# Copying the maxima into the score banks for two key tiles at a time

## What is computed

```python
q = jnp.einsum('bnd,hde->bhne', query, Wq) * scale
k = jnp.einsum('bmd,hde->bhme', query, Wk)
v = jnp.einsum('bmd,hde->bhme', query, Wv)
logits = jnp.einsum('bhne,bhme->bhnm', q, k)
attn = jax.nn.softmax(logits, axis=-1)
out = jnp.einsum('bhnm,bhme->bnhe', attn, v)
```

## Time and profile before

| what | us |
|---|---|
| two timed runs | 1841.31 and 1842.32, median 1841.82 |
| the profiled execution, device time | 1841.39 |
| its span, first to last instruction | 1839.7 |
| PE busy | 1743.4 (95% of the span) |
| POOL busy | 1338.3 (73%) |
| ACT busy | 1318.1 (72%) |
| DVE busy | 1207.4 (66%) |
| granted TensorE clock, mean | 0.994 of full speed |

### The profile page before, as it was taken

One profiled execution on the slowest core, in us unless ns is written; L12 is line 12 of the kernel. 1 busy time (PEld: TensorE's weight loads), 2 busy tenths in 40 slices (PEclk: granted clock), 3 DMA queues, 4 the chain that ended last, 5 costly groups with the idle time before them and its releaser, 6 DMA issues.

```text
span 1839.7 us, 29397 instructions
## 1 busy us (share of the span) xinstructions
PE 1743.4 (95%) x10380; PEld 1074.3 (58%) x10380; DVE 1207.4 (66%) x2155; ACT 1318.1 (72%) x1608; POOL 1338.3 (73%) x711
## 2 busy tenths in 40 slices
PE   7999999999999999999999999999999998999998
PEld 4555555555665555556655555556655454598887
DVE  5666666666676657766665667767666668665565
ACT  3787777776668777776667877776677867665775
POOL 2798888887766867798668778897668787642664
PEclk9999999999999999999999999999999999999999
DMA  4411111113322111133222111132221111543441
GB/s 132 152 47 41 47 41 47 44 57 97 115 78 64 33 41 47 46 105 125 67 67 66 41 44 44 54 106 61 70 69 50 39 58 58 178 121 115 156 138 35
DMA packets 142932, 137.72 MB, mean 75 GB/s; under 512 B 60740, under 2 KB 121284, under 8 KB 141764
## 3 DMA queue, kind: packets, MB, share of 16 engines
q1 hardware_dynamic: 139716, 127.38, 22.9%
q0 software_dynamic: 3072, 8.46, 1.3%
HBM read 102.70 MB, written 29.69 MB: 72 GB/s over the span
## 4 chain that ended last, share of the span: by engine, by line
PE 57%; ACT 12%; POOL 11%; issue 9%; DVE 8%; DMA 2%; SPq 1%; POOLq 0%; ACTq 0%; DVEq 0%
PE av_ps L1200 13%; PE score_ps L1184 11%; POOL prob_sum L1058 9%; PE spare_ps L1160 6%; PE spare_ps L1144 5%; ACT score_ps L1303 4%; PE y_ps L1782 4%; PE spare_ps L441 4%; ACT probs L1295 4%; PE h_ps L1753 4%; PE spare_ps L1137 4%; PE spare_ps L1211 3%; DVE max_of L1361 2%; DVE o_lo L513 2%; DMA x<-x 1%
## 5 line engine op out<-in xcount | busy, mean ns | idle before, releaser
L1058 POOL TENSOR_TENSOR prob_sum<-prob_sum,probs 128x1024 f32<-128x1024 f32 (+1 forms) x384 | 905.4, 2358 | 189.6 <-ACT probs L1295 154.2
L1361 DVE TENSOR_REDUCE max_of<-spare_ps 128x1 f32<-128x512 f32 x1024 | 655.8, 681 | 254.3 <-PE spare_ps L1160 244.7
L1295 ACT ACTIVATE probs<-score_ps 128x1024 f32<-128x1024 f32 x512 | 498.3, 1023 | 326.5 <-PE score_ps L1184 318.7
L1303 ACT ACTIVATE score_ps<-shift_all 128x1024 f32<-128x1024 f32 x510 | 503.7, 1031 | 0.0
L1200 PE MATMUL av_ps<-probs,v 128*64 128x512 f32 x2048 | 488.2, 602 | 0.7 <-DVE sums L1404 0.7
L1160 PE MATMUL spare_ps<-k_hi,q_hi 64*128 64x512 f32 x1024 | 238.4, 456 | 51.2 <-DVE max_of L1361 34.0
L1200 PEld LDWEIGHTS av_ps<-probs,v 128*64 128x64 f32 x2048 | 129.8, 136 | 239.8 <-issue 198.5
L1160 PEld LDWEIGHTS spare_ps<-k_hi,q_hi 64*128 64x128 f32 x1024 | 101.1, 183 | 271.3 <-issue 207.5
L1054 POOL TENSOR_TENSOR prob_sum<-probs 128x1024 f32<-128x1024 f32 (+1 forms) x64 | 150.4, 2350 | 112.1 <-ACT probs L1295 111.9
L1184 PE MATMUL score_ps<-q_hi,k_hi 64*128 64x512 f32 x1024 | 212.0, 406 | 5.9 <-ACT score_ps L1303 5.9
L1184 PE MATMUL score_ps<-q_hi,k_lo 64*128 64x512 f32 x1024 | 204.4, 390 | 0.0
(11 more groups left out here) (279 smaller groups left out, 2298.1 us busy)
## 6 DMA issues: line engine op xcount, KB each, us to landing
shift_all<-shifts SPq DMA_DIRECT2D x64, 512.0 KB, 3.7
o_transposed<-sums SPq DMA_DIRECT2D x64, 256.0 KB, 2.5
v<-in_L_ffn_W_dram SPq DMA_DIRECT2D x16, 1024.0 KB, 5.7
o_in<-o_transposed SPq DMA_DIRECT2D x28, 512.0 KB, 4.1
w_raw<-in_L_attn_Wq_dram SPq DMA_DIRECT2D x64, 64.0 KB, 2.3
w_raw<-in_L_attn_Wk_dram SPq DMA_DIRECT2D x64, 64.0 KB, 2.2
wv_raw<-in_L_attn_Wv_dram SPq DMA_DIRECT2D x32, 128.0 KB, 2.9
shifts<-neg_rows SPq DMA_DIRECT2D x256, 1.0 KB
```

The costliest lines, as they stand in the source:

```text
L1058: pool.tensor_tensor(out, out, probs[:, n % RING, heads], ALU.add).then_inc(prob_added, 1)
L1295: act.activation(probs[:, n % RING], score_ps[n % 2][:, :, :], ACT.Exp).then_inc(probs_ready, 1)
L1303: act.activation(score_ps[n % 2][:, :, :], shift_all[:, u % 2], ACT.Copy).then_inc(seeded, 1)
L1361: dve.tensor_reduce(max_of[:, u % 2, kh, j, hd:hd + 1], bank[:, :], AX.X, ALU.max).then_inc(pass_read, 1)
```

## The change

The table loses one "seed" of two in each place, so that one remains after each pair of exponentials. The two score buffers become halves of one PSUM tensor of four banks. `seed(n)`, called for even n, waits for `probs_ready` n (was n - 1), which is the end of `exp(n - 1)`, the instruction just ahead of it on ACT; it copies the same 1024 maxima twice, 2048 columns in one instruction, into all four banks, and then adds 2 to `seeded`. What `score(n)` waits for is unchanged in the code (`seeded` n - 1). There are 255 such copies in place of 510.

```diff
-    "early av av av pass score score seed seed pass sum av recip pass score score seed seed pass late bite bite",
+    "early av av av pass score score seed pass sum av recip pass score score seed pass late bite bite",
...
-            if name == "seed" and h < HALVES and KT * u + kt + 2 < KT * UNITS:
-                yield "seed", KT * u + kt + 2
+            if name == "seed" and h < HALVES and KT * u + KH * second + 2 * i + 2 < KT * UNITS:
+                yield "seed", KT * u + KH * second + 2 * i + 2
...
-        score_ps = [ctx.enter_context(nc.psum_tensor(f"score_ps{i}", [P, 2, BANK], F32)) for i in range(2)]
+        score_banks = ctx.enter_context(nc.psum_tensor("score_ps", [P, 2, 2, BANK], F32))
+        score_ps = [score_banks[:, i] for i in range(2)]
...
-                act.wait_ge(probs_ready, n - 1)
-                act.activation(score_ps[n % 2][:, :, :], shift_all[:, u % 2], ACT.Copy).then_inc(seeded, 1)
+                act.wait_ge(probs_ready, n)
+                both = shift_all[:, u % 2]
+                act.activation(score_banks[:, :, :, :], bass.AP(both.tensor, both.offset, [both.ap[0], (0, 2), (1, 2 * BANK)]),
+                               ACT.Copy).then_inc(seeded, 2)
```

More of the change, by code:

```diff
@@ L658 @@
 STEPS = tuple(tuple(line.split()) for line in (
-    "early av av av pass score score seed seed pass sum av recip pass score score seed seed pass late bite bite",
-    "bite norm pass score score seed seed pass early av av pass score score seed seed pass late av av",
-    "av pass score score seed seed pass early av sum pass score score seed seed pass bite late av recip av",
-    "pass norm score score seed seed pass early bite bite av pass score score seed seed pass late av av av"))
+    "early av av av pass score score seed pass sum av recip pass score score seed pass late bite bite",
+    "bite norm pass score score seed pass early av av pass score score seed pass late av av",
+    "av pass score score seed pass early av sum pass score score seed pass bite late av recip av",
+    "pass norm score score seed pass early bite bite av pass score score seed pass late av av av"))
 def bites_of(g, quarter, pairs):
```

## The result

| | before | after |
|---|---|---|
| timed runs, median | 1841.82 us | 1916.59 us (1916.56 and 1916.61) |
| ratio | | 1.0408, 95% interval 1.0383 to 1.0433 |
| profiled execution, span | 1839.7 | 1914.9 |
| PE busy | 1743.4 (95%) | 1752.3 (92%) |
| ACT busy | 1318.1 (72%) | 1321.5 (69%) |

The change makes the kernel 4.1% slower, 74.8 us. The forecast was 1915 us. On another chip the changed kernel gave the same ratio, 1.0415 (1.0398 to 1.0432).

What follows compares the result with a forecast made beforehand. PE was taken to bound the attention; +68.8, +3, -2.4, +5.8 and -2 gave +73.2 on the 1839.7 us span, 1912.9, and with 1.7 outside it 1914.6, so 1915 us. Range 1886 to 1936; outer bounds 1891 and 1958.

Steps and rivals of the forecast that it cites:

- The floor: Attention: shortest time between score-pair starts, through scores, exponentials, copy and PE's start, rises from 3.90 to 4.94 us.
- the short windows of A, C and E: Attention stretches between score-pair starts, 29, 32 and 21 windows; with nine others, lifted to 4.94 us, +68.8 us.
- the own wait: On ACT, the merged copy must wait for its last exponential and starts 0.06 us behind it, between -0.11 and +0.12.
- the restart of PE: On PE, the score starts 0.14 us after the copy's end, as read from the trace at 404.20.
- The 66 waits of the weight loads: PE's score weight loads waited 66 times for the copy, 34.3 us; taken as PE and ACT arriving nearly together.
- D: Attention stretch of 5.03 us between score-pair starts; said to fall to 4.94 in 27 places, -2.4 us.
- The chains over ACT: In stretches B and G, work hanging on ACT behind the copy comes 0.09 us later, at most 64 times, +5.8 us.
- The size of the catch-up: Rival: PE's waits for DVE, POOL and `k_lo`, 55 us, are backlogs; 40 us vanish, giving 1875 us; chance 0.07.
- The -2 for POOL: PE's sum waits less for POOL's last add, but only in the few E windows over 4.94 us; -2 us.
- the +3 for the long waits in A: Three A windows near 4.90 us, where PE waited long for the copy, grow by 1.04 us each; +3 us.
- A lasting fall of the clock: Rival: longer PE waits bring one low-clock stretch per cycle, 54 us more, 1969 us; chance 0.05 with like pile-ups.
- the nine short windows: Attention windows under 4.95 us outside kinds A, C and E, 39.72 us together, also lifted to 4.94 us each.

Runs made afterwards that it cites:

- the run with the own wait alone: Kernel before with two copies, each releasing its own buffer; only the first of a pair waits for the exponential just ahead; 1853.72 us, ratio 1.0069.
- The second execution: Second profiled execution of the changed kernel itself, on another chip; its timed run gave 1917.7 us, ratio 1.0415 to the kernel before.
- the late release alone: Kernel before with both copies and old waits; the first copy no longer raises `seeded`, the second raises it by 2; 1893.0 us, ratio 1.0285.

## Why the prediction was right

**The floor.** The step that carried the forecast was to build the shortest chain over ACT with the late release and to lift the short windows of A, C and E onto it. It was forecast at 4.94 and is 4.88 in A: 0.91 + 1.94 + 0.10 + 1.88 + 0.05. So the exponentials were as said, the own wait was 0.10 for 0.06, the copy 1.88 for 1.90 (the price from two shapes held to 1%), and the restart of PE 0.05 for 0.14, the term that was mis-sized.

**What set A before.** The prediction says that the chain over ACT set A at 3.90, and calls it exact. It had to come out exact, since its 0.14 was what was left up to the start at 404.20. PE was busy for all 3.90 us of that A, and two more rows of the kernel before show what it did:

```profile
403.87 0.49 PE L1160 MATMUL spare_ps<-k_hi,q_hi 64*128 64x512 f32 x2
...
404.12 0.19 PEld L1184 LDWEIGHTS score_ps<-q_hi,k_hi 64*128 64x128 f32 x2
```

The score's weights were loaded some 0.05 behind the copy's end (404.06), and its first matmul started about 0.09 later (404.20), behind those of the coarse product ahead. So PE's own work set A, and the copy came with 0.09 to spare; the run with the own wait alone shows it, where the copy ended 0.14 later and A was 0.05 longer. The 66 waits of the weight loads do not show the opposite: 58 of them (23.7 of 34.3 us) stand ahead of the second score of a pair, and the 8 others are the long ones. What they say is only that PE stood ready for the second copy. The forecast did not suffer, since with the late release the chain over ACT is the longer one by far, but the wrong 0.14 came from here.

**The restart.** The missing 0.09 was not saved but moved. Where PE has stood still for the copy, the score's first matmul is shown 0.05 behind it, but the exponential follows 1.00 after that start (426.28 to 427.28) and not 0.91 (421.40 to 422.31), and the second score 0.79 and not 0.71. So a stretch that ends at such a start is 0.09 short, and the next one is 0.09 long. That is most of the error in D (forecast 4.94, measured 5.08 from 438.38 to 443.46, so +1.8 and not -2.4):

```profile
439.39 1.94 ACT L1296 ACTIVATE probs<-score_ps 128x1024 f32<-128x1024 f32 x2 [1.05 <-PE score_ps L1185]
441.44 1.88 ACT L1305 ACTIVATE score_ps<-shift_all 128x2048 f32<-128x2048 f32 x1
```

D is 1.01 + 1.94 + 0.11 + 1.88 + 0.14 = 5.08. It is also why E stands at 4.97, and it is half of the 0.22 by which the typical F grew (+5.5 in all, forecast 0). The other half I had missed: its pass waits for the high part of q, which stands on ACT behind the copy, as k's does in B.

**The chains over ACT.** Forecast were +0.09 in each B and each G. In B the typical cycle did lengthen, from 7.04 to 7.21, by the 0.09 of the restart and about as much of the chain, with PE's wait for `v` now 10.9 us in 18 places (0.7 in 2 before). But three long B stretches (11.14, 11.48 and 11.17 us; the first from 512.04) fell to 10.17, 10.19 and 10.03, 3.4 us in all: with A a microsecond longer ahead of them, PE's wait for `k_lo` in the first, 1.4 us, became one of 0.7 for `v`. The second execution has 10.48 for all three, and two B windows at a granted clock of 0.87 and 0.81 besides, which is where its +2.8 comes from. In G the chain is not to be seen: 22 of the 32 windows are the same within 0.03 us, and the +5.1 lies in a few long ones (one of them 10.29 before and 13.05 after, at a granted clock of 0.83 and 0.74). The forecast's 2.9 for G was right in sign by luck.

**The size of the catch-up.** The -2 for POOL was right for this change. As an account of the kernel it was only half right: merging A and C alone gives back 15.7 us in E. It was right because the floor of E swallowed the rest. The -3.4 in the three long B stretches is catch-up as well, and was not forecast; it cancels the +3 for the long waits in A, which came as said (1.05, 1.03 and 1.32 us).

**The rivals.** That each long copy costs alike is refuted by the late release alone (+52 without one), and by the half of the copies in long stretches that cost 11 us in place of 37. A lasting fall of the clock did not come: the mean granted clock is 0.991 after 0.994, with waits of PE for the copy in 94 places. In the attention the clock stands low in six stretches after, four before; at some 1.7 us each, as in the prediction, up to 3.4 of the 75 us may be the clock's, by this estimate. Merging shortens the copies, 503.7 to 480.0 us, but "ACT's total down by 20 us" failed: ACT's busy time went from 1318.1 to 1321.5, since each first copy had run beside the end of an exponential (0.11 x 255 = 28 us) and now starts behind it. Among kernels that have the late release and the own wait already, merging is worth 8 to 9 us. The prediction calls the rule on guarding PSUM a rule against this change; the change keeps it, since each score still waits for the copy that fills its banks, and what it gives up is time.

**How much of the hit was luck.** The total is right to 2 us, but its terms are not. The forecast was too low by 5.5 us in F, 4.2 in D and 2.2 in G. It was too high by 3.0 in B and 2.0 in A, and its 4.7 for the nine short windows has no measured row of its own: those windows are inside the sums of their kinds. The mechanism and the 62.6 us of A, C and E (65.0 forecast) are the forecast's own; that the rest cancelled is luck. One sum is off: the terms of the upper bound add up to 113, not 116, so it is 1955 and not 1958, and the stated range does not rest on it.

## What to carry to other kernels

When two operations that release two buffers are merged, ask which engine takes the first buffer, and how long it has been waiting at that moment: here its weights were loaded 0.05 us behind the first copy, and the merged operation cost the whole length of its second half, on an engine that was not the bound. Cut the timeline at the point that repeats, compare each stretch with the shortest chain through the other engine, and lift those below the new floor; for the three short stretches that sum was right to 2.4 us in 63, and what fell outside it (the restart, the work queued on ACT behind the copy) was a few us each. Before trusting a gain or a loss from one stretch, look whether another engine's backlog sits in the next one, since it gives back part of a loss as long as that next stretch has no floor of its own.

## What the runs showed of the hardware

A copy on ACT that waits for the exponential just ahead of it starts 0.03 or 0.09 us behind that one's end; without such a wait it overlaps it by 0.11. The length of the copy does not decide between the two. All 255 long copies have their wait as an instruction of its own ahead of them (L1303), and start 0.09 behind in the median. In the run with the own wait alone the same holds for 64 of the 255 first copies of a pair, the very first and those of D and H (L1302); they are short and start 0.09 behind too (334.54, where the exponentials end at 332.48 + 1.96 = 334.44), and the others, whose wait stands on the copy itself, 0.03. What holds for a long copy with its wait on itself was not run. A short copy took 1.02 us in that run where it took 1.03 before.

```profile
L1303 ACTq EVENT_SEMAPHORE  x255: 17/17/38, 42.3 to 1657.3; - x128
```

```profile
L1302 ACTq EVENT_SEMAPHORE  x64: 17/17/17, 43.2 to 1584.3; - x64
```

```profile
332.48 1.96 ACT L1295 ACTIVATE probs<-score_ps 128x1024 f32<-128x1024 f32 x2
334.54 1.98 ACT L1303 ACTIVATE score_ps<-shift_all 128x1024 f32<-128x1024 f32 x2
```

PE starts a score 0.05 us behind the end of the copy that it stood waiting for, and the exponential behind it follows 1.00 after that start, against 0.91 where PE had not stood: the sum from the copy's end is what to reckon with, 1.05 us.
